# Permuting the edge list by one matrix product instead of two

## The reference, cut to what matters

```python
edge_index = jnp.stack([src, dst])
h = jnp.maximum(_layernorm(x, axis=-1), 0.0)
x = x + _L0_gnn_ref(h, L0_gnn_W_lin, L0_gnn_W_agg, edge_index)
...                                   # _L1 (SAGE and a dense chain), _L2, in the same way
h = jnp.maximum(_layernorm(x, axis=-1), 0.0)
x = x + _L3_gnn_ref(h, edge_index, ...)   # attention over the edges, in both directions
# inside _L0 to _L2:
summed = jax.ops.segment_sum(x[src], dst, num_segments=n)   # a sum over the edges of each node
```

## Time and profile before

| what | value |
|---|---|
| time, median of 3 runs | 3301.39 us (3297.81 to 3304.03) |
| time of the profiled execution | 3297.36 us |
| its span, first to last instruction | 3295.5 us |
| busy: PE, DVE, ACT, POOL | 67%, 67%, 26%, 50% of the span |
| mean granted clock of TensorE | 0.828 of full speed |
| first mask of the permutation (L486) | at 131.75 us |
| first read of its result (L501) | at 358.41 us |

### The profile page before, as it was taken

The page is one execution under the profiler, slowest core; times in us unless marked ns, Lnnn a source line. Parts: engine busy times, 40 slices in busy tenths (PEclk is TensorE's granted clock), DMA queues, the critical chain, the costliest instruction groups (busy, mean ns, idle before and its releaser), DMA issues.

```text
span 3295.5 us, 47742 instructions
## 1 busy us (share of the span) xinstructions
PE 2192.3 (67%) x12658; PEld 1222.6 (37%) x12659; DVE 2205.0 (67%) x3520; ACT 847.4 (26%) x1397; POOL 1638.3 (50%) x1455
## 2 busy tenths in 40 slices
PE   0488888887959799994962444444566666638563
PEld 0233343333434355543551111111466511118563
DVE  8999888887468600255043444445987799989777
ACT  0099533331001300022000111111344322206342
POOL 7400133332077777777005777777877777710000
PEclk9899999999989899997975565555559999955897
DMA  2000011112435344301905434435358733530453
GB/s 72 0 0 0 25 50 50 50 50 73 154 83 171 81 96 101 56 1 22 192 20 110 112 112 116 115 112 102 93 164 270 237 112 111 100 33 0 141 178 91
DMA packets 195115, 301.52 MB, mean 91 GB/s; under 512 B 120540, under 2 KB 133818, under 8 KB 194922
## 3 DMA queue, kind: packets, MB, share of 16 engines
q1 hardware_dynamic: 138986, 175.88, 17.0%
q0 software_dynamic: 40512, 62.87, 10.6%
q10 hardware_dynamic: 15552, 61.94, 6.0%
HBM read 191.65 MB, written 88.01 MB: 85 GB/s over the span
## 4 chain that ended last, share of the span: by engine, by line
PE 38%; POOL 20%; issue 17%; DVE 14%; DMA 5%; ACT 5%; ACTq 1%; DVEq 0%; SPq 0%; POOLq 0%; PEldq 0%
POOL arena L1294 19%; PE PS L536 13%; PE PS L680 9%; PE PS L865 6%; DMA arena<-T_att,idx 4%; ACT arena L512 4%; PE PS L962 3%; PE PS L474 2%; PE PS L949 1%; DVE arena L1185 1%; DVE arena L372 1%; DVE arena L558 1%; DVE arena L488 1%; PE PS L1231 1%; DVE arena L557 1%
## 5 line engine op out<-in xcount | busy, mean ns | idle before, releaser
L1294 POOL DMA_INDIRECT arena<-T_att,idx x864 | 844.9, 978 | 314.0 <-issue 228.8
L536 PE MATMUL PS<-arena 128*128 128x400 f16 (+2 forms) x4320 | 760.9, 321 | 238.9 <-issue 131.1
L1129 DVE TENSOR_REDUCE arena<-PS 128x1024 f32 (+1 forms) x432 | 506.6, 1249 | 317.0 <-PE PS L1096 317.0
L536 PEld LDWEIGHTS PS<-arena 128*128 128x128 f16 (+2 forms) x4320 | 452.2, 137 | 538.0 <-issue 346.9
L1467 POOL DMA_INDIRECT order<-arena x400 | 505.6, 1264 | 249.5 <-issue 249.5
L1096 PE MATMUL PS<-arena,pick 128*128 128x512 bf16 x864 | 335.1, 493 | 140.7 <-DVE arena L1129 136.3
L680 PE MATMUL PS<-arena 128*128 128x512 f16 (+1 forms) x1575 | 318.0, 361 | 88.3 <-issue 75.2
L557 DVE TENSOR_SCALAR arena<-arena 128x512 f16<-128x512 f16 x448 | 275.7, 615 | 62.6 <-PE PS L536 61.6
L1085 PE MATMUL PS<-ident_b,score_buf 128*32 128x128 bf16 x864 | 90.0, 267 | 301.4 <-ACT score_buf L1058 292.1
L614 POOL TENSOR_TENSOR rdeg<-rdeg,arena 128x1600 f32<-128x1600 f32 x48 | 154.3, 3216 | 265.1 <-ACT arena L598 265.1
L680 PEld LDWEIGHTS PS<-arena 128*128 128x128 bf16 x1575 | 147.8, 99 | 254.6 <-issue 103.1
(11 more groups left out here) (259 smaller groups left out, 2914.8 us busy)
## 6 DMA issues: line engine op xcount, KB each, us to landing
spill<-arena SPq DMA_DIRECT2D x108, 560.0 KB, 2.9
arena<-spill ACTq DMA_DIRECT2D x108, 560.0 KB, 3.7
arena<-A SPq DMA_DIRECT2D x50, 800.0 KB, 4.5
A<-arena SPq DMA_DIRECT2D x50, 400.0 KB, 2.4
arena<-A SPq DMA_DIRECT2D x50, 400.0 KB, 3.2
arena<-T_att,idx POOLq DMA_INDIRECT x864
order<-arena POOLq DMA_INDIRECT x400
T_att<-h SPq DMA_DIRECT2D x2, 1600.0 KB, 13.3
```

The costliest lines, as they stand in the source:

```text
L536: return t.matmul(where, lhsT, rhs, start=False, stop=True, skip_group_check=True)
L1129: v.tensor_reduce(cmax[d][:, u:u + 2, bass.ds(i * SLOTS + half * GROUP + q // 2 * QUAD, QUAD)], PS[:, u * BANK:(u + 2) * BANK].rearrange(" ...
L1294: p.indirect_dma_start(out=ring1[:, b, j, :], out_offset=None, in_=T_att[d][:, :], in_offset=bass.IndirectOffsetOnAxis(ap=idx[:, d, k:k + ...
```

## The change

The two payloads go through one product. `dst` within its half (0 to 1599) becomes a signed number between 1024 and 2047: 1024 + v for v below 1024, and -(1024 + v - 1024) for the others, which float16 holds exactly. It stands in the moving operand of 448 columns (L486's successor multiplies it in), as its own sign and ten lower bits. `src` within its tile (0 to 127) becomes a power of two, 2^(src - 64), made by shifting an exponent into place, and stands in the stationary operand, now bfloat16. So one float32 in PSUM holds both: its exponent is the source, its sign and ten bits are the destination. (`sort_v[:, 3]` is `power`; `less`, the negated power, is computed too, but nothing reads it.) ACT takes no part: DVE makes both operands of every column, each by an instruction with two scalar operands per partition. PE waits for DVE's `eq_ready` and has one product per column.

```diff
-        ACT_COLS = 3
-        sort_v = view(23200, 4 * EC, EP).rearrange("p (a b) -> p a b", a=4)
+        sort_v = view(23200, 5 * EC, EP).rearrange("p (a b) -> p a b", a=5)
-        B0 = view(3584, 16 * P, EP).bitcast(F16).rearrange("p (g j k c) -> p g j k c", g=4, j=U0, k=2)
-        eq0 = view(5632, 8 * P, EP).bitcast(F16).rearrange("p (g j c) -> p g j c", g=4, j=U0)
+        B0 = view(3584, 8 * P, EP).bitcast(BF16).rearrange("p (g j c) -> p g j c", g=4, j=U0)
+        bits_i = view(5632, 2 * CH[1]).bitcast(I32).rearrange("p (a k) -> p a k", a=2)
+        SHIFT, BIAS, UNIT = 64, 127, 1024
...
-            a, b, v0, v1 = (sort_v[:, i, :] for i in range(4))
+            a, b, v0, power, less = (sort_v[:, i, :] for i in range(5))
...
                 dve_link(v.tensor_scalar(ev_i[:, 0, :], src_i, P - 1, None, ALU.bitwise_and))
-                v.tensor_scalar(v1, ev_i[:, 0, :], 1.0, None, ALU.add)
+                dve_link(v.tensor_scalar(ev_i[:, 0, :], ev_i[:, 0, :], float(BIAS - SHIFT), None, ALU.add))
+                v.tensor_scalar(power.bitcast(I32), ev_i[:, 0, :], 23, None, ALU.logical_shift_left)
                 dve_link(v.scalar_tensor_tensor(v0, ev_i[:, 1, :], -float(BW), dst_i, ALU.mult, ALU.add))
-                dve_link(v.tensor_scalar(v0, v0, 1.0, None, ALU.add))
+                v.tensor_scalar(less, power, -1.0, None, ALU.mult)
+                dve_link(v.tensor_scalar(a, v0, float(UNIT), None, ALU.is_ge))
+                dve_link(v.scalar_tensor_tensor(v0, a, -float(UNIT), v0, ALU.mult, ALU.add))
+                dve_link(v.tensor_scalar(a, a, -2.0, 1.0, ALU.mult, ALU.add))
+                dve_link(v.scalar_tensor_tensor(v0, v0, float(UNIT), a, ALU.add, ALU.mult))
...
                 for j in range(U0):
                     c = bass.ds((4 * i + g) * U0 + j, 1)
-                    v.tensor_scalar(A0[g][:, j, :], steps_h[0:EP, 0:CH[1]], sort_v[:, 0, c], None, ALU.is_equal)
-                    if j < ACT_COLS:
-                        last = v.tensor_scalar(eq0[:, g, j, :], steps_h[0:EP, 0:P], sort_v[:, 1, c], None, ALU.is_equal)
-                    else:
-                        for k in range(2):
-                            last = v.tensor_scalar(B0[:, g, j, k, :], steps_h[0:EP, 0:P], sort_v[:, 1, c],
-                                                   sort_v[:, 2 + k, c], ALU.is_equal, ALU.mult)
+                    last = v.tensor_scalar(A0[g][:, j, :], steps_h[0:EP, 0:CH[1]], sort_v[:, 0, c], sort_v[:, 2, c],
+                                           ALU.is_equal, ALU.mult)
+                    last = v.tensor_scalar(B0[:, g, j, :], steps_h[0:EP, 0:P], sort_v[:, 1, c], sort_v[:, 3, c],
+                                           ALU.is_equal, ALU.mult)
                 last.then_inc(eq_ready, 1)
...
-            v.tensor_scalar(key[:, 1, :], PS[:, 5 * BANK:5 * BANK + CH[1]], -1.0, None, ALU.add)
-            v.tensor_scalar(dst_in, PS[:, 4 * BANK:4 * BANK + CH[1]], -1.0, None, ALU.add).then_inc(sorted_ready, 1)
-        def permute_act(a):
...
+            found = PS[:, 4 * BANK:4 * BANK + CH[1]]
+            v.tensor_scalar(bits_i[:, 0, :], found.bitcast(I32), 23, 255, ALU.arith_shift_right, ALU.bitwise_and)
+            v.tensor_scalar(bits_i[:, 1, :], found.bitcast(I32), 13, UNIT - 1, ALU.arith_shift_right, ALU.bitwise_and)
+            dve_link(v.tensor_scalar(dst_in, found, 0.0, None, ALU.is_lt))
+            v.tensor_scalar(key[:, 1, :], bits_i[:, 0, :], -float(BIAS - SHIFT + 10), -1.0, ALU.add, ALU.max)
+            v.scalar_tensor_tensor(dst_in, dst_in, float(UNIT), bits_i[:, 1, :], ALU.mult, ALU.add) \
+                .then_inc(sorted_ready, 1)
 
         def permute_pe(t):
-            for k in (4, 5):
-                clear_bank(t, k)
+            clear_bank(t, 4)
             with t.Fori(0, LAPS0) as i:
                 for g in range(4):
-                    t.wait_ge(payload_ready, 4 * i + g + 1)
+                    t.wait_ge(eq_ready, 4 * i + g + 1)
                     for j in range(U0):
-                        for k in range(2):
-                            at = (4 + k) * BANK
-                            last = add_to(t, PS[:, at:at + CH[1]], B0[:, g, j, k, :], A0[g][:, j, :])
+                        last = add_to(t, PS[:, 4 * BANK:4 * BANK + CH[1]], B0[:, g, j, :], A0[g][:, j, :])
                     last.then_inc(perm0_used, 1)
...
-            permute_act(a)
```

More of the change, by code:

```diff
@@ L274, in gnn_kernel @@
         placed, addr_ready = sem("placed"), sem("addr_ready")
-        eq_ready, payload_ready, perm0_used = sem("eq_ready"), sem("payload_ready"), sem("perm0_used")
+        eq_ready, perm0_used = sem("eq_ready"), sem("perm0_used")
         sorted_ready = sem("sorted_ready")
@@ L500, in permute_dve @@
             v.wait_ge(perm0_used, 4 * LAPS0)
-            v.tensor_scalar(key[:, 1, :], PS[:, 5 * BANK:5 * BANK + CH[1]], -1.0, None, ALU.add)
-            v.tensor_scalar(dst_in, PS[:, 4 * BANK:4 * BANK + CH[1]], -1.0, None, ALU.add).then_inc(sorted_ready, 1)
-        def permute_act(a):
[L506 to L509, removed]
-                        for k in range(2):
-                            c = bass.ds((4 * i + g) * U0 + j, 1)
-                            last = a.activation(B0[:, g, j, k, :], eq0[:, g, j, :], ACT.Copy, scale=sort_v[:, 2 + k, c])
-                    last.then_inc(payload_ready, 1)
+            found = PS[:, 4 * BANK:4 * BANK + CH[1]]
[5 more added lines that the diff above has]
+                .then_inc(sorted_ready, 1)
         def permute_pe(t):
-            for k in (4, 5):
-                clear_bank(t, k)
+            clear_bank(t, 4)
             with t.Fori(0, LAPS0) as i:
                 for g in range(4):
-                    t.wait_ge(payload_ready, 4 * i + g + 1)
+                    t.wait_ge(eq_ready, 4 * i + g + 1)
                     for j in range(U0):
-                        for k in range(2):
-                            at = (4 + k) * BANK
-                            last = add_to(t, PS[:, at:at + CH[1]], B0[:, g, j, k, :], A0[g][:, j, :])
+                        last = add_to(t, PS[:, 4 * BANK:4 * BANK + CH[1]], B0[:, g, j, :], A0[g][:, j, :])
                     last.then_inc(perm0_used, 1)
```

## The result

The changed kernel takes 3323.24 us (median of 4 runs, 3321.83 to 3325.56), the one before 3300.59 (4 runs). The ratio is 1.0069 [1.0051, 1.0086], that is 17 to 28 us more. The forecast was 3322.2.

A forecast was written before the change was run, and what follows sets the result against it. DVE's own pace was taken to bound the permutation, which the matrix build and all layers await. Terms 18.6 + 1.8 - 2.6 + 1.5 + 1.5 = +20.8 us on the median 3301.39 gave 3322.2 us, range 3309 to 3340.

The forecast's parts named there:

- The bound: In the permutation, DVE sets the pace, ACT follows it and PE follows ACT; 0.479 us per column before.
- The columns: Permutation's masks: 0.527 us per column after the change, wide form 0.305 plus narrow 0.222; +18.6 us.
- a ladder of 0.06 us per scalar read: DVE masks: fixed parts 0.068, 0.130 and 0.189 us with no, one and two scalars read; wide form 0.305.
- the free scalar: Rival: second scalar free on DVE's wide instruction, which stays at 0.246 us; total -2.5, 3299 us; 7%.
- the halved rate: Rival: multiply halves the wide instruction's rate, 0.389 us; columns +51.8, 3355 us; 10% with the narrow-rate case.
- the delayed issue: Rival: in the loop, a second scalar address from a register adds 0.03 us per wide instruction; +12, 3334 us; 5%.
- Ahead: Before the permutation (L428 to L433): added small DVE instructions cost net 2.28 us, 0.5 to spare; +1.8 us.
- The tail: Permutation's end: ACT's step goes, PE's last group is four products instead of eight; 1.2 us instead of 3.8, -2.6.
- The term of +0.7: Part of the clock term: PE's low clock lengthens the permutation's tail by up to +0.7 us.
- Behind: After the permutation, reading and unpacking the result from PSUM: 2.69 us against 1.19; +1.5 us.
- PE's clock: PE's clock may fall; hidden inside the permutation, shows in tail and build's first products; 0 to +3, taken +1.5 us.
- The end: Whole kernel: the terms sum to +20.8 us, passed on to the end; 3322.2 us, slower by 0.6%.

The follow-up runs named there:

- the second profile of the changed kernel: The changed kernel unaltered, run and profiled again against the kernel before: ratio 1.0060 [1.0047, 1.0074], 19.1 us more.

## Why the prediction was right, point by point

- **The bound.** DVE's own pace set the permutation, ACT and PE followed. Shown: taking 0.06 us off each wide instruction of DVE shortened the stretch by 24 us, while doubling PE's products left the pace of the masks as it was.
- **The columns.** 0.305 for the wide form from a ladder of 0.06 us per scalar read; measured 0.31, and 18.8 us against 18.6. (POOL's stretch let 12 masks start and not 11, and lasted 33.1 us against 32.8 from the first mask; these small misses cancel.) That it is the read and not the second operation was argued from three rows and is now shown. The rivals of the free scalar and of the halved rate are out; so is the delayed issue, since the columns of the first lap, whose scalars have constant addresses, show the same 0.306 and 0.223 us as those of the loop.
- **Ahead.** +1.8 for +1.9 in the profile; the start itself scatters by 1.5 us.
- **The tail.** -2.6 forecast. In the second profile of the changed kernel the last group met the full clock: 1.0 us from last mask to first read, -2.8. In the first it met the low one: 1.8, -2.0. The term of +0.7 for that was right.
- **Behind.** +1.5 for +1.5.
- **PE's clock.** The term that was wrong in part. Of the +1.5, the tail is 0.7, as measured in the first profile, and the rest lay in the build's first products. They cost at most 0.1: I had read that PE bounds the build there, but it has up to 1.3 us to spare in a lap of 7.7 (above), and the low clock went into that.
- **The end.** 20.8 forecast, 22.7 and 19.1 measured, 20.2 and 18.3 of it at the build's start. The mechanism up to the build is right to within the scatter of the start. That the end agrees to 1 us is partly luck, since the later stages move it by more than that, and the part of the clock term that was wrong happens to be made up by what they add.

## What to carry to other kernels

Price a short VectorE instruction from start to start and split it: here 0.07 us, 0.26 ns per 16-bit element, and 0.06 us for every scalar that it reads per partition. Fewer instructions were no gain here, where each reads one scalar more, and halving the work of an engine that is not the bound (PE's products) buys only what its last group takes, 0.8 us here (1.69 for eight products, 0.93 for four, at the full clock). What leaves an engine at its limit decides: the same packing gave +0.7% with the work on DVE and -0.7% with half of the narrow operands on ACT.

## What the runs showed of the hardware that was not expected

- POOL's six passes hold DVE's fast masks almost whole (11 started in 32.6 us), while DVE does the same work, in five passes, in 14.3 us. Moving them was worth 17 us.
- The same kernel code reaches its first mask 1.5 us earlier or later, and between 2300 and 2850 us POOL falls behind by 1 to 6.5 us more than in the profile before, whether the kernel was changed or only delayed. A profile's end is thus no measure of a change of a few microseconds; the shift at the next stage's start is.
- PE's loop over eight chunks takes 7.7 to 7.8 us whether its products last 6.40 or 7.37 us, so a low clock at its start does not show in the time.
